# Cross-attention stage: the biases of the MLP's second matrix added by GpSimd to the normed rows, in place of a two-row product on TensorE

## What is computed

```python
z = self_attn(x, Wq1, Wk1, Wv1)
x = layer_norm(x + z, ln1_g, ln1_b)
z = cross_attn(x, context, Wq2, Wk2, Wv2)
x = layer_norm(x + z, ln2_g, ln2_b)
z = jax.nn.relu(x @ fc1_w + fc1_b)
z = z @ fc2_w + fc2_b
return layer_norm(x + z, ln3_g, ln3_b)
```

## Time and profile before

| | |
|---|---|
| median of 3 runs | 1837.16 us (1835.31 to 1838.54) |
| the profiled execution's own time | 1834.65 us |
| its span in the profile | 1832.8 us |
| PE busy | 1714.0 us (94%), 7838 matmuls |
| DVE busy | 913.7 us (50%) |
| ACT busy | 531.2 us (29%) |
| POOL busy | 328.3 us (18%) |
| chain that ended last | PE 84%, DVE 9%, issue 2%, ACT 2%, DMA 1%, POOL 1% |
| cross-attention stage, by the stretches read | about 780 to 1106 us |

### The profile page before, as it was taken

The page is one execution under the profiler, slowest core; times in us unless marked ns, Lnnn a source line. Parts: engine busy times, 40 slices in busy tenths (PEclk is TensorE's granted clock), DMA queues, the critical chain, the costliest instruction groups (busy, mean ns, idle before and its releaser), DMA issues.

```text
span 1832.8 us, 22184 instructions
## 1 busy us (share of the span) xinstructions
PE 1714.0 (94%) x7838; PEld 1385.4 (76%) x7838; DVE 913.7 (50%) x1810; ACT 531.2 (29%) x933; POOL 328.3 (18%) x500
## 2 busy tenths in 40 slices
PE   6797999997989999889999979999999999999999
PEld 5586788875777888667777757787878787878787
DVE  3465654446466545456767776634343434343411
ACT  3231212112212111246556533322222222222222
POOL 0111110002011001035566652000000000000000
PEclk9799999998989999979999989999999999999999
DMA  4211211113021111444444423210101010101000
GB/s 133 103 53 36 80 35 52 35 34 104 26 63 59 46 35 35 129 155 147 149 143 152 149 86 133 61 43 1 47 1 46 1 46 1 46 1 46 1 24 23
DMA packets 68870, 117.38 MB, mean 64 GB/s; under 512 B 11233, under 2 KB 13281, under 8 KB 68603
## 3 DMA queue, kind: packets, MB, share of 16 engines
q1 hardware_dynamic: 64013, 108.34, 18.2%
q10 hardware_dynamic: 4744, 7.58, 1.3%
HBM read 81.05 MB, written 34.84 MB: 63 GB/s over the span
## 4 chain that ended last, share of the span: by engine, by line
PE 84%; DVE 9%; issue 2%; ACT 2%; DMA 1%; POOL 1%; DVEq 0%; SPq 0%; ACTq 0%; POOLq 0%
PE banks L582 78%; PE banks L592 3%; PE banks L706 2%; DVE split_q L1361 1%; DVE small L1667 1%; DVE split L1361 1%; ACT split_q L933 1%; PE banks L793 1%; DVE plain L1416 1%; DVE split L1827 1%; ACT split L933 1%; DVE plain L1854 1%; DVE small L1410 0%; DMA plain<-in_x 0%; DMA plain<-in_L_xattn_Wk 0%
## 5 line engine op out<-in xcount | busy, mean ns | idle before, releaser
L582 PE MATMUL banks<-split 128*128 128x512 f32 (+4 forms) x2292 | 558.1, 394 | 42.6 <-DVE split L1361 24.1
L582 PE MATMUL banks<-split_q,split 128*128 128x512 f32 x2304 | 572.3, 398 | 4.4 <-DVE split_q L1458 4.4
L582 PEld LDWEIGHTS banks<-split 128*128 128x128 f32 (+3 forms) x2292 | 420.7, 190 | 150.0 <-DVE split L1361 26.8
L582 PEld LDWEIGHTS banks<-split_q,split 128*128 128x128 f32 x2304 | 431.2, 190 | 103.1 <-issue 15.2
L582 PE MATMUL banks<-split,split_q 128*128 128x512 f32 (+3 forms) x1824 | 419.9, 384 | 7.5 <-DVE split_q L1361 3.0
L582 PEld LDWEIGHTS banks<-split,split_q 128*128 128x128 f32 x1824 | 329.2, 192 | 67.7 <-issue 5.6
L1361 DVE TENSOR_TENSOR split<-banks,split 128x512 fp32r<-128x512 f32 (+5 forms) x234 | 148.9, 641 | 189.9 <-ACT split L933 189.2
L1231 POOL TENSOR_TENSOR small<-small 128x1 f32<-128x1 f32 (+1 forms) x104 | 29.5, 283 | 1167.9 <-DVE small L1412 595.2
L933 ACT ACTIVATE split<-banks 128x512 fp32r<-128x512 f32 (+5 forms) x234 | 126.4, 557 | 363.4 <-PE banks L706 229.7
L1827 DVE TENSOR_TENSOR split<-plain,split 128x512 fp32r<-128x512 f32 x128 | 89.2, 697 | 226.5 <-ACT split L1202 226.5
L1196 ACT ACTIVATE plain<-banks,small 128x512 f32<-128x512 f32 x128 | 88.0, 687 | 301.9 <-PE banks L582 301.9
(11 more groups left out here) (142 smaller groups left out, 1173.3 us busy)
## 6 DMA issues: line engine op xcount, KB each, us to landing
plain<-in_x SPq DMA_DIRECT2D x56, 256.0 KB, 3.0
xo_scratch<-plain SPq DMA_DIRECT2D x32, 256.0 KB, 3.3
x_scratch<-plain SPq DMA_DIRECT2D x32, 256.0 KB, 2.0
plain<-x_scratch SPq DMA_DIRECT2D x32, 256.0 KB, 2.9
tile_x<-xo_scratch SPq DMA_DIRECT2D x32, 256.0 KB, 3.1
xg_scratch<-tile_x SPq DMA_DIRECT2D x32, 256.0 KB, 2.0
out<-plain SPq DMA_DIRECT2D x32, 256.0 KB, 2.1
tile_x<-x_scratch SPq DMA_DIRECT2D x28, 256.0 KB, 4.5
```

What stands on the lines that cost most here:

```text
L582: mm = nc.tensor.matmul(out, left(c, l), right(c, r), start=start and c == 0 and (l, r) == PASSES[0], stop=stop and c == chunks - 1 and (l ...
```

## The change

The matmul of line 793 is gone, with the rows that it read and their preparation. The bias row (`ln2_b + fc2_b`, now kept in `vec2[:, 3]` over all 128 partitions) is added to the block in `N` by a new GpSimd instruction, `bias_x2(t, k)`, behind `gain_x2(t, k)`, and `add_y(t, k)` waits for it in place of the gain.

```diff
-        y_rows, y_ones = R[0:2, 61 * KB:63 * KB], R[0:2, 63 * KB:63 * KB + P]
-        y_low = R[0:2, 32 * KB:34 * KB]
...
-            sp.wait_ge(y_rows_lo, 1)
-            sp.dma_start(y_rows[1:2].bitcast(F32), y_low[1:2].bitcast(F32)).then_inc(y_rows_in, 16)
...
-                nc.tensor.matmul(PS[:, 4 + k % 2], y_ones, y_rows, start=True, stop=False)
...
-                            start=False, stop=f == C - 1)
+                            start=f == 0, stop=f == C - 1)
...
-            act.wait_ge(vec2_ready, 2)
-            nc.scalar.activation(y_rows, vec2[0:2, 0], copy).then_inc(y_rows_hi, 1)
...
-            act.wait_ge(y_rows_in, 16)
...
+            def bias_x2(t, k):
+
+                pool.wait_ge(x2_gained, t * BT + k + 1)
+                nc.gpsimd.tensor_tensor(N[:, t % 2, k], N[:, t % 2, k], vec2[:, 3], ALU.add).then_inc(x2_biased, 1)
+
...
             gain_x2(0, 1)
+            pool.wait_ge(vec2_ready, 2)
+            bias_x2(0, 0)
+            bias_x2(0, 1)
...
                     rstd_of_h0(0, 3)
+                    bias_x2(t, 2)
+                    bias_x2(t, 3)
                     root_y(t, 0)
...
                     root_z(t + 1, k)
+                bias_x2(t, 2)
                 root_y(t, 0)
                 lo_w(2 * t + 1)
+                bias_x2(t, 3)
                 root_y(t, 1)
                 gain_x2(t + 1, 0)
                 gain_x2(t + 1, 1)
                 root_y(t, 2)
+                bias_x2(t + 1, 0)
+                bias_x2(t + 1, 1)
...
-                dve.wait_ge(x2_gained, t * BT + k + 1)
+                dve.wait_ge(x2_biased, t * BT + k + 1)
...
-            nc.vector.tensor_tensor(vec2[:, 0], vec2[:, 0], vec2[:, 1], ALU.add).then_inc(vec2_ready, 1)
+            nc.vector.tensor_tensor(vec2[:, 3], vec2[:, 0], vec2[:, 1], ALU.add).then_inc(vec2_ready, 1)
...
-            dve.wait_ge(y_rows_hi, 1)
-            nc.vector.tensor_tensor(y_low, vec2[0:2, 0], y_rows.bitcast(F32), ALU.subtract).then_inc(y_rows_lo, 1)
```

More of the change, by code:

```diff
@@ L323, in build @@
         b1_full, b1_ready = sem("b1_full"), sem("b1_ready")
-        y_rows_hi, y_rows_lo, y_rows_in = sem("y_rows_hi"), sem("y_rows_lo"), sem("y_rows_in")
         rows_loaded, rows_hi, rows_lo = sem("rows_loaded"), sem("rows_hi"), sem("rows_lo")
@@ L327, in build @@
         y_full, y_free = sem("y_full"), sem("y_free")
-        x2_gained, xg_ready = sem("x2_gained"), sem("xg_ready")
+        x2_gained, x2_biased, xg_ready = sem("x2_gained"), sem("x2_biased"), sem("xg_ready")
         xo_in = [sem(f"xo_in_{k}") for k in range(BT)]
@@ L863, in step2 @@
                     pe.wait_ge(fcw_lo, 2 * C)
-                    pe.wait_ge(y_rows_in, 16)
                 mlp_out(t, 0)
@@ L1599, in _ @@
             nc.vector.tensor_copy(sum2[:, 0:1], len2[:, 0:1]).then_inc(len_seen, 1)
-            p0.done(nc.vector.memset(y_ones.bitcast(F32), 1.0))
             p2 = Steps(dve, dve_p2)
```

## The result

The changed kernel takes 1822.41 us (median of 4 runs, 1819.57 to 1823.50), against 1836.29 us of the kernel before (median of 4 runs, one more than stand behind the 1837.16 us given ahead of the prediction; 1835.31 to 1838.54). The ratio is 0.9915, with a 95% interval of 0.9899 to 0.9930: 13.9 us less. The forecast was 1823.2 us, 14.0 us less than 1837.16.

What follows compares the result with a forecast made beforehand. TensorE was taken to bound tiles 0 to 5, other engines the stretch after. The terms 14.2 - 1.2 - 0.3 + 1.3 = 14.0 us, taken from 1837.16, gave 1823.2 us, range 1818.5 to 1831.5.

Steps and rivals of the forecast that it cites:

- TensorE bounds tiles 0 to 5: Tiles 0 to 5: TensorE, busy 173.35 of 174.50 us, sets the pace, so removing its matmuls shortens the program.
- The price of a two-row matmul: Behind transposes in tiles 0 to 5: 0.59 us for each of 24 matmuls, 14.2 us in all.
- only its columns: Rival: the delay before the product stays, each removed matmul gives 0.2375 us in tiles 0 to 5; 1831.2 us, chance 0.07.
- The additions' place in GpSimd's idle time: Four additions a tile, 5.2 to 7.0 us, fall into GpSimd's waits before `root_y`; only `bias_x2(t, 3)` is not covered.
- Collisions with VectorE: Additions over `scale_y` and `shift_y` of blocks 0 and 2: up to four collisions of 0.85 us, 3.4 us per tile.
- The stall of 0.2 us a tile: Tiles 0 to 5: collisions that come through cost 1.2 us in all, bounds 0 and 6.6.
- just covers it: Before `softmax(t+1)`: 1.40 us of VectorE idle time plus 0.43 us more, against two collisions of 0.85 us.
- Tile 6: VectorE's chain from `add_y(6, 2)` on: TensorE's gain at most 0.3 us, collisions delay it; net -0.3 us.
- Tile 7: Matmuls of k = 0 and 1 give about 0.9 and 0.8 us, an `h_shift` collision costs 0.4; net +1.3 us.
- Tile 0: The preparation and the two additions before tile 0 lie beside TensorE's first product and cost nothing.
- the sum of 14.0 us: Whole kernel: 14.2 - 1.2 - 0.3 + 1.3 us saved, for 1823.2 us; the forecast's own chance was 0.70.

Runs made afterwards that it cites:

- the kernels with 64 and 65 rows: Kernel before, its two-row matmul kept but made taller with zero rows: 1838.20 us with 64 rows, 1825.42 with 65.
- the kernel with both: Kernel before with its two-row matmuls kept and the 32 GpSimd additions put in as well: 1839.78 us against 1837.35, ratio 1.0017.

## Why the prediction was right

- **TensorE bounds tiles 0 to 5**: right. Four matmuls less took 2.49 us off each of tiles 1 to 5, and TensorE stayed busy 99% of them.
- **The price of a two-row matmul**, 0.59 us from the starts in the earlier trace rows: measured 2.49 / 4 = 0.62. The 12 us between the kernels with 64 and 65 rows show that the gap in front of and behind it belonged to it and not to the start of a product; the rival "only its columns" (0.24) is out, and its number is the price of the same matmul with 65 rows or more, 0.23. So 0.03 us too little for each, 0.8 in tiles 0 to 5. The formula of the Trainium skill ("TensorE: Matmul & The Clock Gate", "Back-to-back issue gap"), in which the rows do not appear, gives about 216 ns for 512 columns. The 0.23 us for 65 rows or more come near it; the 0.62 us for 64 rows and fewer between full ones do not.
- **The additions' place in GpSimd's idle time**: right; doubling them shows where that ends.
- **Collisions with VectorE**: three of the four occur where I put them, at 0.4 us (`shift_y(t, 0)`), 1.0 (`scale_y(t, 2)`) and 0.2 (`shift_y(t, 2)`, 0.95 at 882.74), not 0.85 each; `scale_y(t, 0)` takes 0.3 us more, but it starts over `lo_w`. VectorE has (133.03 - 123.43) / 5 = 1.9 us more a tile, not 3.4. The stall of 0.2 us a tile that I subtracted, 1.2 us in all, did not come from them: the tile takes 32.41 us against 32.40 without additions, and 34.90 in the kernel with both. What I had called "just covers it" was so: of 1.40 us ahead of `softmax`, 0.15 are left. One collision did come through, in the second profile only and at a place that I had not named, `scale_w` behind a late transfer: 1.3 us in one tile, of which the runs without additions show 0.6 to 0.7 for the transfer alone.
- **Tile 6**: I gave -0.3 us. From the start of tile 6 (1022.70 before, 1013.46 after) to the release of TensorE (1054.79 and 1045.69) are 32.09 and 32.23 us, so -0.14. By the run without additions, this is 0.6 us gained from the matmuls and 0.6 given back by the additions. TensorE's wait there is unchanged:

```profile
1045.69 10.10 PE L577 MATMUL banks<-split,split_q 128*128 128x512 f32 x36 [2.04 <-DVE plain L1648]
```

- **Tile 7**: I gave +1.3. From that release to line 1827's part of the first block of the last stage it took 1105.70 - 1054.79 = 50.91 us before and 1094.34 - 1045.69 = 48.65 after, so +2.3 in this pair. In the second profile of the change it took 1091.52 - 1041.90 = 49.62 us, so +1.3. One transfer of codes on this chain landed after 3.89 us in the one and 5.42 in the other, so the size of this term is not known better than that.
- **Tile 0**: I put nothing beyond its four matmuls. In the profile after, the product of 812.34 us took 5.46 us at a mean granted clock of 0.50, the 1.2 GHz level throughout (4.57 us at 0.61 before), and line 1618 took 1.50 us instead of 0.48, over `lo_hid`. In the second profile of the change neither is so (4.47 us at 0.63, and 0.48), and tile 0 gave 2.5 us like the others (809.00 to 849.42, before 808.45 to 851.41). That is one execution against another, not the change.

That the sum of 14.0 us met the measured 13.9 so closely is luck. The errors of the terms all point one way: 0.8 us too little from the price, 1.2 from the stall, 0.2 from tile 6 and up to 1.0 from tile 7. With the terms as measured (14.9, 0, -0.1, and 1.3 to 2.3) the sum is 16.1 to 17.1 us. The medians give 13.9 on one chip and 15.1 on the other. What the profiles show beside the terms is losses that I had put at nothing: the start of 812.34 us and 1.8 us of tile 0 in the one, 0.5 us of a later start and the tile of 33.73 us in the other. They differ from execution to execution by as much as my errors, and the account is closed only to within 2 or 3 us.

One number of the prediction is slightly off in its own terms: 1837.16 - 16.9 - 1.5 is 1818.8, not 1818.5.

## What to carry to other kernels

The price of a matmul in a row is the distance between starts around it, and a short one between tall ones cost more than a tall one in its place: here 0.62 against 0.23 us. Before moving such a product to another engine, try it with zero rows up to more than 64: that alone gave 12 of the 14 us. When work goes to a second engine, add up that engine's idle pieces one by one and the idle pieces of the engine that shares its accesses; four additions a tile were free or nearly so here, eight made a kernel slower than before. And look at what the shorter path leaves uncovered: here it is the transfer of codes, which cost a tile nothing at 34.9 us and up to 0.7 us by itself at 32.4.

Do not take a sum that meets the median as proof of its terms. Here each term had to be read from the trace again, and none was too large.

## What the runs showed of the hardware

A matmul of 2, 32 or 64 rows and 512 columns between ones of 128 rows costs the same, 0.62 us, and one of 65 costs what one of 128 does, 0.23 us; the edge lies between 64 and 65 rows. Behind the small one the next weights are loaded later (0.43 us from load to load instead of 0.11), and ahead of the small one's own load the weight load is idle for 0.17 us; a second small one behind the first has no such delay (0.11 us from load to load).

An addition of 128x512 float32 on GpSimd took 1.26 to 1.29 us by itself. Beside it a VectorE operation with two inputs in SBUF took up to 1.78 us where it took 0.74 or 0.75 alone, and the addition 1.68 to 1.75.
